# A graph network layer on one core: root in batches on VectorE, biases written into PSUM by ScalarE, and a reordered head

## The reference

```python
def layer(h, src, dst, distances, fw1, fb1, fw2, fb2, pw, pb, mw1, mb1, mw2, mb2):
    centers = jnp.linspace(0.0, 10.0, 50)
    rbf = jnp.exp(-(distances[:, None] - centers) ** 2 / (2.0 * width * width))
    cut = 0.5 * (jnp.cos(jnp.pi * distances / 10.0) + 1.0) * (distances <= 10.0)
    W = (silu(rbf @ fw1 + fb1) @ fw2 + fb2) * cut[:, None]
    messages = (h[src] @ pw + pb) * W
    agg = segment_sum(messages, dst, num_segments=12500)
    return h + (silu(agg @ mw1 + mb1) @ mw2 + mb2)

x = layernorm(x + layer(x, src, dst, edge_weight, ...))   # eps 1e-5, over the 128 features
```

## Time and profile before

| | us |
|---|---|
| median of 3 runs | 1214.91 (1213.65 to 1217.35) |
| the profiled execution | 1215.85, its span 1214.1 |
| PE busy | 661.1 (54%) |
| POOL busy | 617.6 (51%) |
| DVE busy | 579.6 (48%) |
| ACT busy | 346.4 (29%) |
| granted TensorE clock, mean | 0.735 |

### The profile page before, as it was taken

The page is one execution under the profiler, slowest core; times in us unless marked ns, Lnnn a source line. Parts: engine busy times, 40 slices in busy tenths (PEclk is TensorE's granted clock), DMA queues, the critical chain, the costliest instruction groups (busy, mean ns, idle before and its releaser), DMA issues.

```text
span 1214.1 us, 12087 instructions
## 1 busy us (share of the span) xinstructions
PE 661.1 (54%) x3533; PEld 569.2 (47%) x3593; DVE 579.6 (48%) x2078; ACT 346.4 (29%) x485; POOL 617.6 (51%) x688
## 2 busy tenths in 40 slices
PE   3943820572855138337454545747556766655673
PEld 3833720461745027226343435636455655544562
DVE  5654920481964038248533533974264343324443
ACT  2941400330422023113222032402233334333332
POOL 2136777126275731733663626674456565655651
PEclk9976765695777558668775767778677877867786
DMA  4944242021114121202142212313132222331110
GB/s 161 317 126 128 55 129 54 16 69 45 46 49 114 52 74 26 76 24 65 49 125 76 61 33 70 88 46 95 56 84 72 70 74 73 90 81 54 46 50 33
DMA packets 56693, 92.63 MB, mean 76 GB/s; under 512 B 12901, under 2 KB 32038, under 8 KB 56618
## 3 DMA queue, kind: packets, MB, share of 16 engines
q1 hardware_dynamic: 37450, 52.08, 14.2%
q0 software_dynamic: 19168, 39.68, 12.9%
HBM read 75.34 MB, written 16.37 MB: 76 GB/s over the span
## 4 chain that ended last, share of the span: by engine, by line
another core or an unknown queue 33%; DVE 24%; PE 18%; issue 11%; ACT 9%; DMA 2%; DVEq 1%; POOL 0%; SPq 0%; ACTq 0%; POOLq 0%
PE ps_sum L728 5%; PE ps_w L719 5%; DVE agg L1090 5%; DVE pairs L908 4%; PE ps_h L710 3%; DVE message L1074 3%; ACT act_t L614 2%; DVE member L1068 2%; ACT L614 2%; ACT L609 2%; ACT square L606 1%; DVE move L906 1%; ACT rbf L609 1%; DVE moves_now L904 1%
## 5 line engine op out<-in xcount | busy, mean ns | idle before, releaser
L513 POOL DMA_INDIRECT gathered<-proj_rows,src_tab x564 | 556.1, 986 | 234.6 <-issue 165.0
L1074 DVE TENSOR_TENSOR message<-ps_w,gathered 128x512 f32<-128x512 f32 x141 | 97.5, 692 | 385.1 <-remote 237.7
L728 PE MATMUL ps_sum<-member,message 128*128 128x64 f32 x1128 | 188.2, 321 | 162.6 <-DVE message L1074 101.4
L728 PEld LDWEIGHTS ps_sum<-member,message 128*128 128x128 f32 x1128 | 178.4, 239 | 172.5 <-DVE message L1074 110.8
L719 PE MATMUL ps_w<-fw_sb,act_t 128*128 128x128 f32 x1128 | 192.9, 325 | 113.3 <-issue 73.3
L614 ACT ACTIVATE act_t<-ps_h 128x512 f32<-128x512 f32 x141 | 82.2, 596 | 573.1 <-remote 443.3
L1090 DVE TENSOR_TENSOR agg<-agg,ps_sum 128x64 f32 x564 | 122.7, 218 | 186.9 <-remote 128.5
L719 PEld LDWEIGHTS ps_w<-fw_sb,act_t 128*128 128x128 f32 x1128 | 194.5, 242 | 36.1 <-issue 21.4
L710 PE MATMUL ps_h<-rbf,fw_halves 128*128 128x256 f32 x564 | 190.0, 463 | 23.9 <-issue 18.6
L1068 DVE TENSOR_SCALAR member<-iota_f,dst_tab,cut_tab 128x64 f32<-128x64 f32 x564 | 177.0, 322 | 1.1 <-issue 0.7
L716 PEld LDWEIGHTS ps_w<-bias_rhs,one_lanes 128*128 128x128 bf16 x141 | 15.2, 108 | 318.1 <-ACT act_t L614 181.5
(11 more groups left out here) (146 smaller groups left out, 539.9 us busy)
## 6 DMA issues: line engine op xcount, KB each, us to landing
dist_bc<-tile_dist SPq DMA_DIRECT2D x70, 256.0 KB
x_ring<-in_x SPq DMA_DIRECT2D x48, 256.0 KB, 4.5
gathered<-proj_rows,src_tab POOLq DMA_INDIRECT x564
proj_rows<-x_ring SPq DMA_DIRECT2D x24, 256.0 KB, 4.6
out_nodes<-x_ring SPq DMA_DIRECT2D x24, 256.0 KB
pair_rows<-pairs SPq DMA_DIRECT2D x4, 640.0 KB
dist_in<-in_edge_weight SPq DMA_DIRECT2D x5, 312.5 KB
src_in<-in_src SPq DMA_DIRECT2D x5, 312.5 KB
```

Source lines behind the costliest of these rows:

```text
L513: nc.gpsimd.indirect_dma_start(out=gathered[:, slot, :], out_offset=None, in_=proj, in_offset=bass.IndirectOffsetOnAxis(ap=table[:, c:c + ...
L728: last = nc.tensor.matmul(ps_sum[m % 2][:, WINDOW * t:WINDOW * (t + 1)], message[:, m % 2, t * P:(t + 1) * P], member[:, m % 2, t, :], sta ...
L1074: V.tensor_tensor(message[:, n % 2, :], ps_w[n % 2][:, :], gathered[:, MACRO * slot:MACRO * (slot + 1), :].rearrange("p t f -> p (t f)"), ...
```

## The change

It has these parts.

1. **Root.** GpSimd's `scale` is gone. VectorE computes 1/sqrt(var + eps) itself: a first guess from the bits of the float and two Newton steps, for a batch of up to four chunks (`roots`, `ROOTS`). A batch follows its last chunk's statistics by one macro; normalising, storing and reloading follow from `rooted`.
2. **Biases.** The split, the lanes and the bias matmuls are gone. SyncE loads the biases repeated over the 128 lanes, ScalarE writes them into the PSUM bank ahead of the products (`put_bias`), and the products add to them. For the second layer the write of macro m waits for the message of macro m-2, whose bank it takes. TensorE writes the two product banks once at the start.
3. **Head.** VectorE's first group has an order of its own (`prepare_first`): row counts and row search come before most of the shifts, checks and scale constants come after the compaction. TensorE adds the row counts up after chunk 1 in place of chunk 3. ScalarE clears `agg` in five large pieces behind the projections, in place of 25 between them.
4. **Source table.** The table of source rows is made, turned and taken apart from the others (`tables_src`, `turn_src`, `take_src`), at n = 21 in place of 23, and GpSimd waits for it alone.

```diff
+ROOTS = ((0, 4), (4, 8), (8, 12), (12, 16), (16, 20), (20, 23), (23, 24), (24, 25))
+def rooted(i):
+    lo, hi = ROOTS[BATCH_OF[i]]
+    return NODE_AFTER[hi - 1] + 5, i - lo
...
# SyncE
-            for i, b in enumerate((fb2, mb2, pb)):
-                sp.dma_start(bias_in[0:1, i, :], b.rearrange("(a n) -> a n", a=1)).then_inc(biases_loaded, 16)
+            for i, b in ((PB, pb), (FB2, fb2), (MB2, mb2)):
+                sp.dma_start(bias_bc[:, i, :], b.partition_broadcast(P)).then_inc(biases_loaded, 16)
...
-                    if m == after + 9:
+                    if m == at + 4 + place:
                         store_out(i)
...
# GpSimd
-            def scale(i):
-                pool.wait_ge(node_stats, i + 1)
-                step(nc.gpsimd.tensor_tensor(rstd[:, i % RING, :], var_eps[:, i % RING, :], minus_half[:, :], ALU.pow))
-                step(nc.gpsimd.tensor_tensor(shift[:, i % RING, :], minus_mean[:, i % RING, :], rstd[:, i % RING, :],
-                                             ALU.mult))
-                pool.sem_inc(node_scaled, 1)
...
-                    pool.wait_ge(main.tables_ready, k + 1)
+                    pool.wait_ge(main.src_taken, k + 1)
...
# ScalarE
+            def put_bias(out, rows, which):
+                return nc.scalar.activation(
+                    out[0:rows, :].rearrange("p (j f) -> p j f", j=CHUNK),
+                    bias_bc[0:rows, which, :].rearrange("p (j f) -> p j f", j=1).to_broadcast([rows, CHUNK, P]),
+                    ACT.Copy)
...
-                nc.scalar.activation(agg[:, WIDE * i:WIDE * (i + 1)], ones_cols[:, 0:WIDE], ACT.Copy, scale=0.0)\
-                  .then_inc(sums_cleared, 1)
...
+                act.wait_ge(proj_copied, i + 1)
+                if i + 2 < CHUNKS:
+                    put_bias(ps_w[i % 2], chunk_nodes(i + 2)[1], PB)
...
             def silu(p, macro, parity):
+                if p is main:
+                    if macro >= 2:
+                        act.wait_ge(p.msg_ready, macro - 1)
+                    put_bias(ps_w[parity], P, FB2)
                 act.wait_ge(p.h_ready, macro + 1)
...
+                act.wait_ge(node_h_used, i + 1)
+                put_bias(ps_node, chunk_nodes(i)[1], MB2).then_inc(node_act_ready, 1)
...
-                    if m == after + 8:
+                    if m == at + 3 + place:
                         normalise(i)
...
# TensorE
-                nc.tensor.matmul(ps_w[n % 2][:, :], one_lanes[:, 0:P], bias_rhs[:, 0, :, :],
-                                 start=True, stop=False, skip_group_check=True)
...
-                if i == 3:
+                if i == 1:
                     pe.wait_ge(const_built, 3)
                     spread_ends(0)
...
# VectorE
+            def roots(first, chunks):
+                of = slice(first % RING, first % RING + chunks)
                 settle()
-                step(V.tensor_scalar(var_eps[:, i % RING, :], mean_var[:, :, 1], EPS, None, ALU.add))
-                done(V.tensor_scalar(minus_mean[:, i % RING, :], mean_var[:, :, 0], -1.0, None, ALU.mult))
-                dve.sem_inc(node_stats, 1)
+                done(V.tensor_scalar(var_eps[:, of, :], mean_var[:, of, :, 1], EPS, None, ALU.add))
+                done(V.tensor_scalar(root_i[:, of, :], var_i[:, of, :], -0.5, ROOT_MAGIC, ALU.mult, ALU.add))
+                for n, (a, b) in enumerate(ROOT_STEPS):
+                    done(V.tensor_tensor(root_sq[:, of, :], root[:, of, :], root[:, of, :], ALU.mult))
+                    done(V.scalar_tensor_tensor(out=root_sq[:, of, :], in0=root_sq[:, of, :], scalar=b,
+                                                in1=var_eps[:, of, :], op0=ALU.mult, op1=ALU.mult))
+                    done(V.scalar_tensor_tensor(out=rstd[:, of, :] if n else root[:, of, :], in0=root_sq[:, of, :],
+                                                scalar=a, in1=root[:, of, :], op0=ALU.add, op1=ALU.mult))
+                done(V.scalar_tensor_tensor(out=shift[:, of, :], in0=mean_var[:, of, :, 0], scalar=-1.0,
+                                            in1=rstd[:, of, :], op0=ALU.mult, op1=ALU.mult))
+                dve.sem_inc(node_scaled, 1)
...
+            def prepare_first():
+                drop_far(0, 0)
+                dve.wait_ge(const_built, 1)
+                drop_far(0, 1)
+                step(V.memset(before[:, 0:1], 0.0))
+                drop_far(0, 2)
+                dve.wait_ge(const_built, 3)
+                spread_counts(0)
+                build_lanes()
+                shift_by(0)
+                take_ends(0)
+                find_rows(0)
+                for n in range(1, STEPS):
+                    shift_by(n)
+                    if n == 5:
+                        address_pieces(0)
+                clear_empty(0)
+                build_scales()
+                check_pieces(0)
+                select_pieces(0)
+                tables_src(main)
+                tables_angle()
+                take_src(main, 0, 0, GROUP_SIZES[0])
+                tables_cosine()
+                tables_rows(main, 0)
+                take_tables(main, 0, 0, GROUP_SIZES[0])
```

More of the change, by code:

```diff
@@ L67 @@
 NODE_END = MACROS + 10
+ROOTS = ((0, 4), (4, 8), (8, 12), (12, 16), (16, 20), (20, 23), (23, 24), (24, 25))
+BATCH_OF = [next(b for b, (lo, hi) in enumerate(ROOTS) if lo <= i < hi) for i in range(CHUNKS)]
 RING = 8
-N_BIAS = 3
+FB2, MB2, PB = range(3)
+CLEARED = 5
+ROOT_MAGIC = 1595932665.0
+ROOT_STEPS = ((0.703952253 * 2.38924456, -0.703952253), (1.5, -0.5))
 COS = [(-1) ** k / math.factorial(2 * k) for k in range(9)]
@@ L362, in _ @@
             sp.wait_ge(const_built, 1)
-            sp.wait_ge(biases_split, 1)
-            for part in range(3):
-                sp.dma_start(bias_lanes[part:part + 1, :, :], bias_parts[0:1, part, :, :]).then_inc(bias_placed, 16)
             load_edges(1)
@@ L409, in nodes @@
             def nodes(m):
-                for i, after in enumerate(NODE_AFTER):
-                    if m == after + 9:
+                for i in range(CHUNKS):
+                    at, place = rooted(i)
+                    if m == at + 4 + place:
                         store_out(i)
-                    if m == after + 12 and i + RING < CHUNKS:
+                    if m == at + 7 + place and i + RING < CHUNKS:
                         load_x_again(i + RING)
@@ L560, in _ @@
                                 main.gathered[m % SLOT_MACROS])
-            for m in range(MACROS, NODE_END + 4):
-                nodes(m)
             pool.wait_ge(outside_ready, 1)
@@ L575, in _ @@
                                             general.gathered[j])
-                for i in range(CHUNKS, 2 * CHUNKS):
-                    scale(i)
         @block.scalar
@@ L602, in _ @@
                   .then_inc(proj_copied, 1)
+                act.wait_ge(proj_copied, i + 1)
+                if i + 2 < CHUNKS:
+                    put_bias(ps_w[i % 2], chunk_nodes(i + 2)[1], PB)
+            act.wait_ge(const_built, 1)
+            for i in range(CLEARED):
+                n = AGG_COLS // CLEARED
+                nc.scalar.activation(agg[:, n * i:n * (i + 1)].rearrange("p (a n) -> p a n", n=WIDE),
+                                     ones_cols[:, 0:WIDE].rearrange("p (a n) -> p a n", a=1)
+                                     .to_broadcast([P, n // WIDE, WIDE]), ACT.Copy, scale=0.0)\
+                  .then_inc(sums_cleared, 1)
             def radial(p, unit, parity, loads):
@@ L665, in _ @@
             pe.wait_ge(const_built, 2)
+            for b in ps_w:
+                for half in range(2):
+                    last = nc.tensor.matmul(b[:, 2 * P * half:2 * P * (half + 1)], ident_halves[:, 0:P],
+                                            ident_halves[:, 0:2 * P], start=(half == 0), stop=True,
+                                            skip_group_check=True)
+            last.then_inc(banks_marked, 1)
             def turn(i):
@@ L741, in node_second @@
                 rows = chunk_nodes(i)[1]
-                nc.tensor.matmul(ps_node[0:rows, :], one_lanes[:, 0:rows], bias_rhs[:, 1, :, :],
-                                 start=True, stop=False, skip_group_check=True)
                 for t in range(CHUNK):
@@ L939, in address_pieces @@
                 rows = P * min(k + 1, ROW_GROUPS)
-                total = ends[:, rows - 1:rows]
+                step(V.tensor_scalar(row_start[:, :], row_at[:, :], float(ROW_SLOTS), None, ALU.mult))
+                step(V.tensor_tensor(left[:, :], ends[:, rows - 1:rows], first[:, k:k + 1], ALU.subtract))
                 dve.wait_ge(quad_loaded, 16 * (k + 1))
-                step(V.tensor_scalar(splits[:, :], quad[:, :], first[:, k:k + 1], None, ALU.subtract))
-                step(V.tensor_scalar(row_start[:, :], row_at[:, :], float(ROW_SLOTS), None, ALU.mult))
@@ L1209, in _ @@
                     statistics(i)
+                    roots(i, 1)
 DVE_GENERAL_STEPS = 57
```

161 lines of the change are left out of this document (72 added, 89 removed).

## The result

The changed kernel took 1279.16 us (1270.72 to 1281.47, four runs) against 1216.13 us for the kernel before (1213.65 to 1225.26, four runs): 1.049 times the time, 95% interval 1.042 to 1.057. It is slower; 1192 was forecast, with a range of 1158 to 1236. The profiled execution took 1281.47 us, span 1279.7, that is 65.6 us more span than before.

| | after, us | before, us | forecast change | measured change |
|---|---|---|---|---|
| to the message of macro 24 | 294.6 | 302.5 | -10 | -8 |
| macros 24 to 52 | 234 | 234 | 0 | 0 |
| 52 to 80 | 253 | 222 | +12 | +31 |
| 80 to 109 | 280 | 212 | +30 | +68 |
| 109 to 125 | 117 | 216 with the next | 96 forecast | |

What follows compares the result with a forecast made beforehand. Late TensorE signals during GpSimd's gather streams were taken to bound the kernel: streams plus what pauses consume. Terms -10 + 0 + 3 + 12 + 30 - 58 = -23 gave 1193 us profiled, 1192 median; own range 1172 to 1210, wider 1158 to 1236.

Steps and rivals of the forecast that it cites:

- The reading of before: Whole kernel: while GpSimd streams gathers, TensorE's signals reach the others late, coming through when the stream pauses.
- rival (c): Whole kernel: nameless waits are unrelated to streams or are late gathers; near 1100 us, chance 0.08.
- 3.2 us after the run: Late in the kernel: VectorE gets TensorE's word 3.2 us after a run of 16 gathers, having waited 11.41 us.
- the price of the two middle stretches: Second and third stretch: unstopped streams of 65 to 70 us at 8.36 us per macro, +12 and +30 us.
- The gathers themselves are then ahead by the ring's 16 macros: After the middle stretches: gathers lead by 16 macros instead of 4, cashed in at the end.
- The last stretch: Last 31 macros: 16 at 6.0 us with four messages per stop, then 15 free at 3.7 to 4.1; -58 us.
- rival (a): Last stretch: ring stops GpSimd too briefly, macros keep 8.36 us; +38 us, 1230 us, chance 0.24.
- Its sign: Ring part of the last stretch: stops of more than 8 us, or fewer than three messages per stop.
- The head: Start of the kernel: VectorE's shorter path to the compacted rows gives -10 us, bounds 0 and -16.
- Bias in PSUM at 0: Macro loop: 141 TensorE bias matmuls go, 141 ScalarE writes come; 0 us, between -20 and +25.
- Roots at +3: Node statistics: roots move from GpSimd to VectorE in 8 batches of 9 steps; +3 us, bounds 0 and +5.

Runs made afterwards that it cites:

- The cap: Changed kernel with GpSimd's lead over the messages limited (16 macros before); late-signal chips: limit 3 took 1019.19 us, limit 4 plus bias matmuls 1014.48 us.
- a_headonly: Changed kernel with loop biases back as bf16 matmuls and roots and stops back on GpSimd, prompt-signal chip: 896.97 us, 0.989 of the kernel before.
- experiment 5: Late-signal chips, changed kernel with GpSimd's lead capped at 3: 1019.19 us, 0.843 of before; capped at 4 with bias matmuls: 1014.48 us, 0.838.
- a_stops: Changed kernel with GpSimd's 25 stops back, root still on VectorE and bias on ScalarE, prompt-signal chip: 868.88 us, 0.956 of the kernel before.
- a_matbias: Changed kernel with message and node biases back as bf16 matmuls on TensorE, prompt-signal chip: 853.05 us, 0.941 of the kernel before.
- T3: Reading that unfinished gathers pile up; tried as changed kernel with a small GpSimd memset behind every main gather: 966.30 us, 1.067 of the kernel before.

## Why the prediction was wrong

**The reading of before was right for the chip that it came from.** Beside long streams of gathers TensorE's signals come late. The cap shows by experiment that long streams cost time, and rival (c), by which streams do no harm, falls on those chips. The rule of the Trainium skill ("SBUF — State Buffer", Who interferes with whom) that a DMA never contends with a compute engine agrees with the traces of the prompt chips. On the late ones TensorE is held beside the streams, but no run shows what holds it, so they do not decide about the rule. In one place the prediction read too much into its rows: "3.2 us after the run" holds for all seven streams of 20 us, but in the earlier trace rows ScalarE's word comes 9.1 us after the end of the stream (219.06 to 228.12), and VectorE had not waited at 1020.04.

**The step that failed is the price of the two middle stretches**, "I price them at the first stretch's 8.36": +12 and +30 were forecast, +31 and +68 measured, 57 of the 89 us by which the sum is off. The length of single streams is not what was missed there: they ran for up to 69 and 74 us, and 65 to 70 were forecast. The longest stream of the trace after (114 us, 315.6 to 429.8) lies in the stretch from macro 24 to 52, which took 234 us in both traces.

```profile
352.80 0.69 DVE L1095 TENSOR_TENSOR message<-ps_w,gathered 128x512 f32<-128x512 f32 x1 [6.65 <-remote]
...
404.65 0.69 DVE L1095 TENSOR_TENSOR message<-ps_w,gathered 128x512 f32<-128x512 f32 x1 [32.00 <-remote]
```

Such a standstill was in the trace before as well, in a stream of 94 us (124.9 to 219.1), which a longest stream of 65 to 70 us overlooks:

```profile
162.02 0.69 DVE L1074 TENSOR_TENSOR message<-ps_w,gathered 128x512 f32<-128x512 f32 x1 [7.05 <-remote]
...
215.47 0.69 DVE L1074 TENSOR_TENSOR message<-ps_w,gathered 128x512 f32<-128x512 f32 x1 [34.82 <-issue]
```

What was missed is the lead. "The gathers themselves are then ahead by the ring's 16 macros" was right at macro 109: 15.5 macros, where it had been 2.5. The forecast cashed this lead in at the end and nowhere paid for it. The 8.36 comes from a stretch in which GpSimd issued the gathers of 28 macros while 28 were consumed. From 80 to 109 it issued 37.5 for 29 consumed. These 8.5 more, at 5.0 us of stream each, are 43 us (an estimate; the streams in this stretch take 192 us in place of 146), and 38 are missing. In the earlier stretches the lead gained nothing: it stands at 7.0 macros at 24, 52 and 80, since VectorE makes the tables and the row search at fixed macros of its own loop, and GpSimd waits for them. From 52 to 80, 28 macros were issued for 28 consumed, at 9.0 us and not 8.36; why the other 19 us came, no run parts.

**The last stretch**: that the lead is cashed in was right, the rhythm wrong. Four messages were to pass for each stop of 4.1 us; GpSimd made nine stops in 16 macros, 36.7 us, that is 4.1 each but only 1.8 messages per stop. (16 x 5.0 + 36.7) / 16 = 7.3 us per macro in place of 6.0, and 16 macros took 117 us, nearly the 7.4 at which rival (a) decides. Its sign, fewer than three messages per stop, is there. And the 15 free ones took 72 us, 4.8 each in place of 4.0. The last gather is at 1178 and not near 1100. Together -27 in place of -58, 31 us more of the 89.

**The head** was right in size: -8 by macro 24 there, -10 by a_headonly on a prompt chip, with what else that keeps. The first gather came at 63.32 (about 64 forecast), but the first message at 85.01 and not near 79: the early gathers delay it (an argument), which the prediction had named as a bound; where signals are prompt it comes at 77.72.

**Bias in PSUM at 0**: no run parts the write from its wait. The new wait was called harmless because TensorE's word on message m-2 comes first. That overlooked that message m-2 is VectorE's, and late when VectorE is: 198.5 us of waits at L586, and 12 us of time on prompt chips once GpSimd is relieved. Under a cap on late chips it can't be told from nothing (experiment 5).

**Roots at +3**: about right for VectorE (its busy time rose by 5.8 us in all) and wrong in kind. The 49 us that GpSimd spends in and around L540 and L541 count nearly in full as soon as GpSimd sets the time, -44 on prompt chips. The prediction looked at them as stops only, since in its trace GpSimd had time to spare.

**What stays open.** How much of the 65.6 us comes from the missing stops and how much from the wait at L586 was not parted on a late chip: a_stops and a_matbias both ran elsewhere. With the before trace's rate for each row of the table above, the messages outside streams would take 421 us and not 452; so some 30 us (an estimate) are not explained by the streams' length, and the wait at L586 may be in them. T3, the pace of the gathers, was tried only where signals are prompt. And it is open why chips differ. One trait goes with it: a macro's four gathers end in 64 completion signals, and the traces with prompt signals have on average 64 such records per macro, those with late signals 12 to 19, though the gathers' packets end as quickly (about 1 us after the issue in both). That points at the path of signals and of their records, not at the transfers, but it is an argument and no experiment. The Trainium skill ("NOTIFIC — Programmer's Manual", When the ring fills) says that a queue of such records can be set to drop new ones, overwrite old ones or stall the engine that sends them; whether anything like the last is at work no run here shows. Every time in this document is that of an execution whose span and clock were recorded. So a rival stands untested: that the recording itself slows TensorE on the late kind, and that the kernel runs there as elsewhere when nothing is recorded.

## What to carry to other kernels

A profile holds for the kind of chip it was taken on. Before a long wait that no instruction explains is taken as a law of the hardware, run the unchanged kernel on another chip; here it decided the sign. And a lead that a ring buffer permits is not a gain in itself: whoever counts what it gives at the end has to count the time in which it is built up. A cap of 4 macros cost nothing where signals are prompt; where they are late, the changed kernel took 16% less than the kernel before with a cap of 3, and also with one of 4 and bias matmuls. An operation taken off an engine is worth its whole time only where that engine sets the pace, so say for each stretch which engine that would be if the largest unexplained wait were gone.

## What the runs showed of the hardware

- The same program takes 905 to 908 us on five chips and 1206 to 1216 on two and in the comparison of the result, its executions within 1.1% of the median of each.
- On the late kind, TensorE issues and signals slowly well into a stream of indirect gathers from GpSimd: matmuls 2.80 us apart, a signal 23.9 us late. Messages nearly stop beyond 30 us of stream (2 in 153 us before, 6 in 285 after). ScalarE's waits end 3.1 to 3.3 us after a stream of 20 us (seven times before), but 8.0 to 9.1 us after four of 69 to 114 us; one of 63 us let it through before its end. ScalarE's own steps are not slower (0.60 us for the activation in both).
- On the prompt kind a stream of 755 us of such gathers, or 221 MB of traffic at eight or nine tenths of the transfer engines, leaves no "remote" wait.
- An indirect gather costs GpSimd 977 to 1003 ns in the mean of a trace, without a split between the kinds, and 0.30 us between two.
